# A two-layer graph network on one core: a new order for layer 1's turn, one table-driven loop over its steps, and layer 0's h2 in PSUM

## The reference, cut to what matters

```
x = layernorm(x + L0(x)); x = layernorm(x + L1(x))
L0: h = leaky([x_dst, x_src - x_dst] @ W1 + b1); h = leaky(h @ W2 + b2)
    out[n] = sum of h over the edges with dst == n
L1 (attention, 4 heads, with self loops):
    z = (x @ W) per head;  logit = leaky(a_src[src] + a_dst[dst], 0.2)
    alpha = softmax of the logits over the edges of one dst
    out[n] = mean over heads of sum(alpha * z[src]) + bias
```

## Time and profile before

| what | us |
|---|---|
| median of 3 runs | 8767.18 (8765.54 to 8771.23) |
| the profiled execution's own time | 8752.71 |
| its span, first to last instruction | 8751.0 |
| busy PE / DVE / ACT / POOL | 6087.3 / 5776.1 / 3928.5 / 6087.9 |
| mean granted TensorE clock | 0.876 |

### The profile page before, as it was taken

One profiled execution on the slowest core, in us unless ns is written; L12 is line 12 of the kernel. 1 busy time (PEld: TensorE's weight loads), 2 busy tenths in 40 slices (PEclk: granted clock), 3 DMA queues, 4 the chain that ended last, 5 costly groups with the idle time before them and its releaser, 6 DMA issues.

```text
span 8751.0 us, 204204 instructions
## 1 busy us (share of the span) xinstructions
PE 6087.3 (70%) x46823; PEld 4733.0 (54%) x46824; DVE 5776.1 (66%) x13889; ACT 3928.5 (45%) x10077; POOL 6087.9 (70%) x6281
## 2 busy tenths in 40 slices
PE   6777777777777777775466666666666666666667
PEld 5656666666666666564344444444444444444446
DVE  5555555555555555555577777777777777777777
ACT  4444444444444445443344444444444444444443
POOL 4777777777777777774777767677676767766650
PEclk8888888888888888886799999898998989899898
DMA  3111111111111111112111111111111111111110
GB/s 100 40 40 40 40 40 40 40 40 40 40 40 40 40 40 40 40 40 37 30 30 29 28 27 27 27 27 28 26 28 27 27 27 28 28 27 27 27 22 15
DMA packets 276883, 301.80 MB, mean 34 GB/s; under 512 B 169511, under 2 KB 173108, under 8 KB 276566
## 3 DMA queue, kind: packets, MB, share of 16 engines
q0 software_dynamic: 200704, 265.33, 16.2%
q1 hardware_dynamic: 74082, 32.92, 1.5%
q10 hardware_dynamic: 2068, 3.20, 0.1%
HBM read 286.33 MB, written 16.30 MB: 35 GB/s over the span
## 4 chain that ended last, share of the span: by engine, by line
POOL 31%; issue 23%; DVE 21%; PE 14%; DVEq 4%; ACTq 2%; POOLq 2%; ACT 2%; DMA 0%; SPq 0%
POOL big L406 31%; PE ps L993 6%; DVE S L509 6%; PE pu L979 4%; DVE state L709 2%; POOLq L397 2%; DVE rowA L658 1%; DVE rel L506 1%; DVE rowD L663 1%; DVE Y L690 1%; DVEq L725 1%; ACT ST L1197 1%; DVE zz L730 1%; ACTq L258 1%; DVE mnew L750 1%
## 5 line engine op out<-in xcount | busy, mean ns | idle before, releaser
L406 POOL DMA_INDIRECT big<-x_dram,idx x3136 | 3095.8, 987 | 1365.6 <-issue 975.3
L406 POOL DMA_INDIRECT big<-q_dram,idx x3136 | 2991.0, 954 | 1041.6 <-issue 1041.6
L979 PE MATMUL pu<-Y,S 128*128 128x265 f32 x7856 | 2142.9, 417 | 739.7 <-DVE Y L690 734.7
L979 PEld LDWEIGHTS pu<-Y,S 128*128 128x128 f32 x7856 | 1494.8, 200 | 1031.4 <-issue 783.5
L690 DVE TENSOR_TENSOR Y<-big,ps 128x1040 f32<-128x1040 f32 x982 | 1210.7, 1233 | 658.6 <-ACT ps L1201 572.4
L509 DVE TENSOR_TENSOR S<-ps,rel 128x1024 f32 x978 | 1197.8, 1225 | 222.1 <-DVE rel L506 222.1
L1098 ACT COPY ST<-ps 128x512 bf16<-128x512 bf16 x978 | 537.5, 585 | 1489.0 <-PE ps L871 1489.0
L885 PE MATMUL pu<-rowX,S 128*128 128x192 bf16 x3936 | 587.5, 285 | 852.5 <-SPq L330 679.3
L546 DVE TENSOR_TENSOR Y<-Y,rowX 128x512 f32<-128x512 f32 x491 | 340.6, 694 | 1143.4 <-ACT rowX L1110 1139.8
L885 PEld LDWEIGHTS pu<-rowX,S 128*128 x3936 | 395.7, 102 | 1011.6 <-issue 922.0
L993 PE MATMUL ps<-identb,S 128*128 128x128 bf16 x3912 | 550.0, 231 | 526.1 <-DVE S L509 524.4
(11 more groups left out here) (176 smaller groups left out, 8465.6 us busy)
## 6 DMA issues: line engine op xcount, KB each, us to landing
big<-q_dram,idx POOLq DMA_INDIRECT x3136
big<-x_dram,idx POOLq DMA_INDIRECT x3136
rowD<-dst_dram SPq DMA_DIRECT2D x196, 32.0 KB
x_dram<-big SPq DMA_DIRECT2D x7, 483.0 KB, 6.2
idx<-srcT_dram SPq DMA_DIRECT2D x98, 32.0 KB, 1.8
dstc<-dstT_dram SPq DMA_DIRECT2D x98, 32.0 KB
q_dram<-state SPq DMA_DIRECT2D x2, 1536.0 KB, 9.6
out<-big SPq DMA_DIRECT2D x6, 448.0 KB
```

The source lines that it names most:

```text
L406: nc.gpsimd.indirect_dma_start(o, None, x_dram if l else q_dram, bass.IndirectOffsetOnAxis(ap=idx[:, half, t:t + 1], axis=0)).then_inc(gat ...
L979: last = t_.matmul(bank, Sf[:, t, :], Y[:, t, :], start=(t == 0), stop=(t == 7))
```

## The change

It has these parts.

1. **Layer 1's order.** On DVE: y0 (2 turns ago), nz, nl, np, mnew, dd (3 ago), y1 (2 ago), old and acc (both 3 ago; acc was 4 ago), adx, zz, lz, dw (1 ago), then rel and S of this step, last. On ACT: ST (now 1 ago), e, mb, tm, sf0, w, sf1 (now 1 ago). On PE: sums0, ad (now 1 ago), sums1, transposes of this step last.
2. **The loop.** `Steps.run` has one loop over all steps of a super group. Each entry of the table now holds, for step n, the block in the low 10 bits of entry i of the old kind and the group of step i above it. In each turn each engine calls `advance`, which loads the next step's entry, checks its bounds, shifts it and keeps the group in a register; the row in the super group and the block follow by two subtractions. On DVE `advance` stands behind S.
3. **The table** is made at the start: two small DMAs read the groups' first destinations again, across partitions; DVE compares each group's last step number with all 490 step numbers (4 comparisons of 128x490), and PE counts by 4 matmuls with a column of ones before it starts with the node features; DVE adds the counts, shifted, to Bt.
4. **Layer 0.** h2 is a PSUM bank (ps1). The transposes of S all go to bank ps0 and ACT copies them at once, as layer 1 does. DVE waits for layer 0's preparation to have read its last bank before it clears them. A wait for `lo` is put ahead of the write of h2.
5. POOL reads a table entry by `block_of`, with one more register operation to mask the block.

```
+            def advance(self, sn):
+                v = self.eng.value_load(Bt[0:1, ds(sn + 1, 1)], min_val=0, max_val=G << SHIFT | (NB - 1))
+                self.eng.reg_mov(self.group, self.eng.scalar_reg_alu(ALU.logical_shift_right, v, SHIFT))
+
+            def run(self, l, i, turn, arrive=None):
+                eng = self.eng
+                apart(eng)
+                end = eng.snap(block_of(eng, self.last, i * GS + (AHEAD + GS)) + (i * GS + GS))
+                lo = eng.snap(self.first, min_val=0, max_val=STEPS - 1)
+                with eng.Fori(lo, end) as n:
+                    sn = eng.snap(n, min_val=0, max_val=STEPS - 1)
+                    g = eng.snap(self.group, min_val=0, max_val=G - 1)
+                    if arrive is not None:
+                        arrive(g)
+                        apart(eng)
+                    eng.reg_mov(self.row, g - i * GS)
+                    eng.reg_mov(self.at, sn - g)
...
+                    turn(k)
+                eng.reg_mov(self.first, end)
```

DVE's turn of layer 1, the end of it:

```
+                        k.after("adx", 1)
                         v.tensor_tensor(zz[:, 0], g1[:, ds(here, TG), D + 1:XW], adx[:, :, :], ALU.add)
...
                     if k.has(0):
                         k.after("sf1", 2)
                         onehot(k, half, (k.sn % 2) * TG)
-                    if k.has(2):
-                        weigh(k, 1, at)
-                    if k.has(3):
-                        ab = acc[:, ds(b, 1), :, :].rearrange("p b h d -> p (b h) d")
-                        k.after("e", 3)
-                        v.tensor_tensor(ab, ab, ee[:, 0, :].unsqueeze(2).to_broadcast([P, H, D + 1]), ALU.mult
-                                        ).then_inc(m["old"], 1)
-                    if k.has(0):
+                        k.advance()
                         tiles.push(k.r * TG + half * TS)
                         blocks1.push(k.b)
```

PE's turn of layer 1:

```
             def turn(k):
                 if k.has(2):
                     k.after("tm", 4)
                     sums(k, 0)
+                if k.has(1):
+                    dests = adp[:, ds(pe_blocks.back(1 - max(k.tail, 0)), 1), :, :].rearrange("p b k h -> p (b k h)")
+                    k.after("adx", 2)
+                    k.after("sts", 1)
+                    for t in range(TG):
+                        last = t_.matmul(ps[2][:, t * 3 * H:(t + 1) * 3 * H], ST[:, t, :], dests,
+                                         start=True, stop=True)
+                    last.then_inc(L[1]["ad"], 1)
+                if k.has(2):
+                    sums(k, 1)
                 if k.has(0):
                     k.after("S", 0)
...
                     last.then_inc(L[1]["stp"], 1)
+                    k.advance()
+                    pe_blocks.push(k.b)
```

ACT's turn of layer 1 (`ends(k, h)` makes Y's extra columns and the f32 copy of S, which is the stage sf of half h):

```
                 def turn(k):
-                    if k.has(2):
-                        ends(k, 1, 2)
+                    if k.has(1):
+                        k.after("stp", 1)
+                        a_.copy(ST[:, :, :], ps[0][:, :].bitcast(bf16).rearrange("p (t n) -> p t n", t=TG)
+                                ).then_inc(m["sts"], 1)
...
                     if k.has(1):
-                        ends(k, 0, 1)
-                    if k.has(0):
-                        k.after("stp", 0)
...
+                        ends(k, 0)
+                        k.after("dw", 1)
                         k.after("y1", 2)
                         a_.activation(wb[:, :, :], dw[:, :, :], ACT.Exp).then_inc(m["w"], 1)
+                        ends(k, 1)
                     if k.has(0):
+                        k.advance()
                         act_tiles.push(k.r * TG + half * TS)
                         act_blocks.push(k.b)
```

More of the change, by code:

```diff
@@ L44 @@
 PAST = AHEAD + 1
+TABLE = max(AHEAD + G + 1, STEPS + 1)
+SHIFT = 10
 BF = 3 * D
@@ L250, in apart @@
             eng.sem_inc(idle, 1)
[L252 to L264, removed]
@@ L549, in turn0 @@
                 return turn
-            first0 = first_block(dve, "first0")
+            walk0 = Steps(dve, "walk0")
             def steps0(i, q, half):
                 dve.wait_ge(dst_in[half], (q + 1) * 16)
-                steps(dve, 0, i, first0, turn0(half))
+                walk0.run(0, i, turn0(half))
                 dve.sem_inc(fredge_flatd, 1)
@@ L629, in _ @@
             link(v.memset(rowR[:, GE:GE + 1], -BIG))
+            link(v.memset(ps[0][:, :], 0.0))
             link(v.memset(ps[2][:, :], 0.0))
@@ L775, in steps1 @@
                 dve.wait_ge(dst_in[half], (q + 1 + (NS - NS // 2 if half == 0 else NS // 2)) * 16)
-                steps(dve, 1, i, first1, turn1(half))
+                walk1.run(1, i, turn1(half))
                 dve.sem_inc(fredge_flatd, 1)
@@ L824, in _ @@
             pe.wait_ge(s["idn"], 2)
+            pe.wait_ge(s["bt"], 1)
+            for c in range(4):
+                last = t_.matmul(ps[2][0:1, 0:TABLE], one[:, :], later[:, c, :], start=(c == 0), stop=(c == 3))
+            last.then_inc(s["gt"], 1)
             def index_rows(k, q):
@@ L921, in turn0 @@
                 return turn
-            first0 = first_block(pe, "pe_first0")
+            walk0 = Steps(pe, "pe_walk0")
             def steps0(i, q, half):
-                steps(pe, 0, i, first0, turn0(half), lambda g: pe.wait_ge(ready, g + 1))
+                walk0.run(0, i, turn0(half), lambda g: pe.wait_ge(ready, g + 1))
             pe.wait_ge(s["b2in"], 16)
             pe.wait_ge(s["idb"], 1)
-            prime(pe, 0, "stp0 stp1 htp z0 z1 U z2")
+            prime(pe, 0, "stp htp z0 z1 U z2")
             pe.sem_inc(gdone, 2)
@@ L994, in turn @@
                     last.then_inc(L[1]["stp"], 1)
-                if k.has(2):
-                    sums(k, 1)
-                if k.has(0):
-                    dests = adp[:, ds(k.b, 1), :, :].rearrange("p b k h -> p (b k h)")
-                    k.after("adx", 1)
-                    k.after("sts", 0)
-                    for t in range(TG):
-                        last = t_.matmul(ps[2][:, t * 3 * H:(t + 1) * 3 * H], ST[:, t, :], dests,
-                                         start=True, stop=True)
-                    last.then_inc(L[1]["ad"], 1)
-            first1 = first_block(pe, "pe_first1")
+                    k.advance()
+                    pe_blocks.push(k.b)
+            walk1 = Steps(pe, "pe_walk1")
             def steps1(i, q, half):
                 turns(i)
-                steps(pe, 1, i, first1, turn)
+                walk1.run(1, i, turn)
             prime(pe, 1, "stp ad U0 U1")
```

187 lines of the change are left out of this document (109 added, 78 removed).

## The result

The changed kernel takes 9616.92 us (median of 4 runs, 9595.15 to 9645.9), the kernel before on the same chip 8766.36 (4 runs, 8754.11 to 8771.23): a ratio of 1.0975, 95% interval 1.0942 to 1.1007. The forecast was 8990 with a range up to 9110. The sign was right, the size was a quarter of what came. The profiled execution took 9645.9 us with a span of 9643.8, 892.8 more than the span of before.

A forecast was written before the change was run, and what follows sets the result against it. Layer 1 was taken as bound by a ring of waits through DVE, PE and ACT, layer 0 by POOL. Steps +119, boundaries +101, start +5 gave +225 on 8752.7: 8978, said as 8990 for the median; range 8700 to 9110.

The forecast's parts named there:

- the mechanism: Layer 1's ring: DVE's wait for w goes, but its sequencer's round after S lies bare by 0.59 us.
- S to y0: DVE in layer 1: the sequencer's round from S to y0 takes 1.73 us, S covering 1.14.
- y0 to adx: DVE's engine work in a layer 1 step, from y0 to adx: 4.42 us.
- adx to S: DVE in a layer 1 step, from adx to the next S: 1.74 us.
- PE's second way from S to adx: Layer 1: transposes, PE's control, sums0 at 3.9 us, ad; adx at 6.15 as on DVE, step 7.9, +119 us.
- the clock's term: PE in layer 1's ordinary steps: no added cost from the lower clock; granted clock taken as 0.91.
- rival D: Layer 1: PE's sums0 meets the lower clock in one step of ten, +88 us, 9080 in all; chance 0.10.
- Boundaries: Between layer 1's super groups: net +2.07 us each, for 49, +101 us.
- The wait before the scan: Layer 1's super group boundary: the 1.02 us wait before L658 goes, as PE reaches maxima's transposes sooner.
- The start: PE's first work waits for the table: between 0 and +12 us, taken as +5.
- block_of on POOL: One more register operation per group, hidden under a running gather: cost 0; 55 us if bare.
- Layer 0: POOL remains the bound; h2 in PSUM, single copy and added waits worth 0 while a step is under 8 us.

The follow-up runs named there:

- The second load: Changed kernel plus a second, unused load of the next table entry on PE's sequencer behind the transposes: 10079.82 us, ratio 1.1515 to the kernel before.
- The filled gap: Changed kernel plus seven bf16 matmuls that nothing reads behind each step's transposes on PE: 9172.92 us, ratio 1.0472 to the kernel before.

## Why the prediction was right and wrong

**Right: the mechanism and DVE's part.** The wait for w is gone, y0 comes after S with bare issue in every step, y1 ends most of POOL's idle time, the sequencer's loads lie on the ring. The chain of waits has the round that was foretold from the earlier trace rows, entry by entry:

```profile
6011.47 0.30 DVEq L279
...
6011.81 0.21 DVEq L279
...
6012.11 0.16 DVEq L280
...
6012.30 0.15 DVEq L217
...
6012.54 0.23 issue
6012.78 0.25 DVEq L287
```

S to y0 is 2.01 us in place of 1.73: 0.43 for the parts not seen together before was 0.28 too little; around the branch 0.23 us of issue is shown, the shift takes 0.16 and the pushes 0.15. y0 to adx without its wait is 4.33 (4.42 predicted), adx to S 1.75 (1.74).

**Wrong, the step that failed: PE's second way from S to adx and its clock.** The prediction put PE's control behind the transposes at "about 1.5 us by the same count" and sums0 at S+3.9, so that both ways met at 6.15. It is 1.94 us of idle weight loads, sums0 starts at S+4.33 and adx at 6.60. Full-clock step 8.36 instead of 7.90: 440 x 0.46 = 200 us. The second load showed that this way counts whole. What the count had wrong is the gap between a sequencer's entries: it took 0.03, read from DVE's list, and PE's is 0.058. From the first entry behind the transposes to sums0 the trace has twelve entries of 1.28 us in all and twelve gaps of 0.73 us in all, 2.00 in place of 1.5. The wider gap alone is 0.33 of that; the branch, 0.22 by itself, is the next largest.

**Wrong, larger: the clock's term was put at nothing in the sum and carried as rival D, with a chance of 0.10 and a fifth of its size.** D had PE "meets its lower level in one step of ten: each adds 1.8 us": 88 us. In the trace it is 440 x (9.425 - 8.36) = 469 us. The price holds for one step wholly at the lower level (sums0 3.73 in place of 2.06, the step +1.84), a mixed one costs 1.3; the number was wrong: three steps in four, not one in ten. The prediction had opened a stretch of 1.5 us on PE in every turn and asked only when PE arrives, not what the clock does there; it took the 0.91 of before as given. The filled gap shows about 450 us of the loss to be this.

**Boundaries:** predicted +2.07, measured +2.84 in the mean. S to the first maxima operation is 1.71 (1.75 predicted), and first y0 to S is 7.39 (7.64): adx starts 5.61 us after the first y0. The prediction had 5.9, but its own terms add up to 1.55 + 3.90 + 0.2 = 5.65; the 0.25 above that came from no row. The wait before the scan did not go:

```profile
4418.84 1.69 PE L1002 MATMUL ps<-ident,edgeA 128*32 128x128 f32 x8 [1.65 <-issue]
```
```profile
4420.56 1.21 DVE L708 TENSOR_TENSOR_SCAN rowA<-rowX,ps 32x512 f32<-32x512 f32 x1 [1.48 <-PE ps L1002]
```

PE has nothing in front of it, but its sequencer still has to leave the loop (1.65 us of issue here, 70.5 us in all 49, where before it was 4.7): DVE comes 0.9 us earlier and waits that much longer. The mean from the first maxima operation to the scan is 3.55 us, before 3.67. Of the 1.02 us only 0.12 went.

**The rest.** The start cost 11.4 us, within 0 to 12 but not the 5 taken; PE's table comes first, at 13.24 us, and its first transposes at 14.96 in place of 10.62:

```profile
13.24 1.79 PE L864 MATMUL ps<-S 128*1 128x490 bf16 x4 [13.24 <-DVE S L483]
14.96 1.06 PE L886 MATMUL ps<-ident,state 128*64 128x128 f32 x4
```

block_of on POOL is free, as predicted: layer 0's idle time is 1052.6 against 1041.6 us, and 955.4 in both without the wait before the first gather (97.2 and 86.2 us). By the same count the gap between two gathers is 0.30 us and not the 0.33 of the prediction, which had that first wait in it. In layer 1 975.3 / 3136 is 0.311, so the gathers need 4071 us and not 4036, and POOL's slack was 302 us and not 337; nothing in the sum hangs on either. Layer 0, put at nothing, became 31.7 us shorter; its slow gathers, 31 us in all, are gone. Which piece of the new layer 0 does that is open.

The sum of what was found, without the clock: steps 440 x (8.38 - 7.69) = +303, boundaries 48 x (23.72 - 21.03) = +129, start +11, layer 0 -32: +411 against 418 measured with the gap filled. The other 459 of the 877 measured in that group are what the filling takes away, 445 of them in the steps.

## What to carry to other kernels

When control is moved behind the last instruction of a ring, count its round on every engine of the ring, add up the idle stretch that it opens on TensorE, and price the matmuls behind that stretch at both clock levels: here the clock's fall cost 450 us, more than the 0.9 us x 440 of the bare rounds themselves. A cheap test is to fill the stretch with matmuls that nothing reads; if the kernel gets faster while its full-clock step stays as long, it was the clock. Put the advancing of registers ahead of the wait that starts the ring's instruction, not behind it: here that took 0.9 us off the step.

## What the runs showed of the hardware

- 3423 useless matmuls made a kernel 459 us (4.8 per cent) faster. With PE standing still for 1.8 us between its 1.1 us of transposes and the sums, three steps in four have the lower granted clock in them (312 mixed and 31 low of 440); with 0.3 us left of that stretch it is 11 of 440.
- A second value load lengthens PE's round by 0.73 us and DVE's by 0.64, though the load itself takes 0.30 on both: check, assertion, a split register operation and a gap behind each entry (0.058 us on PE, 0.035 on DVE) come with it.
- A shorter step with less idle time on PE can still see the granted clock fall more often: 204 times at a full-clock step of 7.40 us against 79 at 7.66.
- 176 of 3136 gathers of layer 0 took over 960 ns (up to 1442) with h2 in SBUF and two copies, 2 to 21 in the nineteen traces with h2 in PSUM and one copy (4 to 8 in the five without stalls); which of the two does it was not tried.
- There are executions in which every version of this program takes 13,268 to 14,139 us, with single waits of up to 17 us (changed kernel), and that on a chip on which the kernel before takes 8,755 us at another time.
